# A new prologue, later expert pairs, other places for the routing sums and a split last out-projection in an attention and MoE kernel

## The reference, cut to what matters

```
xn = layernorm(x)
attn: q, k, v = xn @ W + b; softmax(causal(q k^T / sqrt(128))) v @ W_O + b_O
ffn:  r = rmsnorm(xn, ln1_w); q, k = rope(r @ wq), rope(r @ wk); v = r @ wv
      resid2 = xn + attention(q, k, v) @ wo
      xf = rmsnorm(resid2, ln2_w); probs = softmax(xf @ gate_w.T)
      sel = top_k(probs + bias_e, 4); rw = probs[sel] / max(sum(probs[sel]), 1e-12)
      ffn = resid2 + sum_e rw_e * (silu(xf @ weg_e) * (xf @ weu_e)) @ wed_e + shared expert
out = x + attn + ffn
```

## Time and profile before

| what | us |
|---|---|
| three runs | 790.8, 795.21, 793.09 (median 793.09) |
| profiled execution, its own time | 791.5 |
| its span, first to last instruction | 789.7 |
| TensorE busy | 738.3 |
| VectorE, ScalarE, GpSimd busy | 548.8, 490.2, 477.8 |

### The profile page before, as it was taken

The page is one execution under the profiler, slowest core; times in us unless marked ns, Lnnn a source line. Parts: engine busy times, 40 slices in busy tenths (PEclk is TensorE's granted clock), DMA queues, the critical chain, the costliest instruction groups (busy, mean ns, idle before and its releaser), DMA issues.

```text
span 789.7 us, 14401 instructions
## 1 busy us (share of the span) xinstructions
PE 738.3 (93%) x4629; PEld 661.2 (84%) x4629; DVE 548.8 (69%) x1689; ACT 490.2 (62%) x1230; POOL 477.8 (60%) x552
## 2 busy tenths in 40 slices
PE   1899999999999999999988995999999999999995
PEld 1678888888888888989877885999999999999995
DVE  5878888797878887675788763555555655555575
ACT  3777768777777775666434662556655566555652
POOL 3679676776867684327223774566556675665543
PEclk9999999999999999999999997999999999999999
DMA  5000000100010099201000534566797677776351
GB/s 170 27 15 28 14 15 15 34 15 21 24 45 28 14 308 295 73 14 42 14 28 14 184 110 130 128 142 157 165 266 159 162 163 162 176 173 142 68 133 54
DMA packets 103491, 77.51 MB, mean 98 GB/s; under 512 B 6950, under 2 KB 102266, under 8 KB 103418
## 3 DMA queue, kind: packets, MB, share of 16 engines
q1 hardware_dynamic: 92234, 63.19, 28.1%
q0 software_dynamic: 10752, 12.74, 9.7%
q10 hardware_dynamic: 432, 0.67, 0.3%
HBM read 51.75 MB, written 24.82 MB: 97 GB/s over the span
## 4 chain that ended last, share of the span: by engine, by line
PE 64%; DVE 13%; ACT 9%; POOL 7%; issue 4%; DMA 2%; DVEq 0%; SPq 0%; POOLq 0%; ACTq 0%
PE j L820 17%; PE zb L820 8%; PE ob L820 8%; PE s L820 8%; PE t L955 6%; ACT probs L1103 4%; POOL x_slots_dram L686 4%; PE j L909 4%; DVE probsT L1383 3%; PE zb L909 2%; PE ob L909 2%; PE j L917 2%; ACT rope_swapped L1143 2%; ACT rope_swapped L1144 2%; DVE rope_sum L1415 1%
## 5 line engine op out<-in xcount | busy, mean ns | idle before, releaser
L675 POOL TENSOR_SCALAR probs<-probs,inv_sum 128x128 f32<-128x128 f32 x244 | 141.8, 592 | 166.9 <-DVE inv_sum L1374 162.9
L1103 ACT ACTIVATE probs<-probs,neg_max 128x128 f32<-128x128 f32 (+3 forms) x256 | 143.1, 560 | 126.4 <-DVE neg_max L1368 124.9
L820 PE MATMUL s<-k_heads,q_heads 128*128 128x256 f32 (+2 forms) x576 | 138.1, 360 | 3.4 <-DVE neg_max L1368 2.8
L1368 DVE CUSTOM_DVE_ANT_0 probs<-s,mask 128x128 f32<-128x128 f32 (+3 forms) x256 | 119.9, 484 | 11.7 <-PE s L820 6.6
L711 POOL DMA_INDIRECT moe_sum_dram<-late,slot_tokens x64 | 101.4, 1584 | 38.7 <-ACT late L1188 25.7
L1383 DVE TENSOR_TENSOR probsT<-t,probsT 128x384 fp32r<-128x384 f32 (+2 forms) x192 | 101.1, 547 | 12.7 <-ACT probsT L1118 11.9
L1118 ACT ACTIVATE probsT<-t 128x384 fp32r<-128x384 f32 (+2 forms) x192 | 89.8, 486 | 19.4 <-PE t L955 19.3
L955 PE MATMUL t<-ident,probs 128*128 128x128 f32 x640 | 94.3, 274 | 7.8 <-POOL probs L675 6.5
L820 PEld LDWEIGHTS s<-k_heads,q_heads 128*128 128x128 f32 x576 | 90.9, 189 | 10.2 <-DVE neg_max L1368 6.6
L955 PEld LDWEIGHTS t<-ident,probs 128*128 128x128 f32 x640 | 74.9, 140 | 16.6 <-POOL probs L675 8.6
L820 PE MATMUL zb<-probsT,v_heads 128*128 128x512 f32 (+2 forms) x351 | 68.3, 339 | 1.4 <-DVE probsT L1383 0.9
(11 more groups left out here) (251 smaller groups left out, 1576.9 us busy)
## 6 DMA issues: line engine op xcount, KB each, us to landing
x_slots_dram<-mask SPq DMA_DIRECT2D x1, 8480.0 KB, 38.3
late<-x_slots_dram SPq DMA_DIRECT2D x32, 265.0 KB, 4.5
late<-in_L_ffn_weg_dram SPq DMA_DIRECT2D x64, 128.0 KB
late<-in_L_ffn_weu_dram SPq DMA_DIRECT2D x64, 128.0 KB
late<-in_L_ffn_wed_dram SPq DMA_DIRECT2D x64, 128.0 KB
moe_sum_dram<-mask SPq DMA_DIRECT2D x2, 1152.0 KB, 8.8
raw_qk<-in_L_ffn_wq_dram SPq DMA_DIRECT2D x16, 128.0 KB, 2.2
raw_o<-in_L_ffn_wo_dram SPq DMA_DIRECT2D x8, 256.0 KB, 2.6
```

The lines of the kernel that those rows point to most:

```text
L675: pool.tensor_scalar(piece, piece, rinv[:, u % 2, i:i + 1], 1.0, ALU.mult, ALU.mult).then_inc(p_norm, 1)
L820: m = pe.matmul(dst, lhs(a), rhs(b), start=first and i == 0, stop=last_ and i == 2, skip_group_check=skip)
L1103: act.activation(piece, piece, ACT.Exp, bias=nmax[:, u % 2, i:i + 1], scale=-1.0, accum_out=rsum[:, u % 2, i:i + 1]).then_inc(e_done, 1)
L1368: ve.tensor_tensor_reduce(pr[:, u % 2, P_OFF[i]:P_OFF[i] + width], bS[i % 2][:, 0:width], mask_t[:, S - width:S], INV_SCALE, BIG, ALU.add, ...
```

## The change

**Prologue.** SP loads x of batch 0, then the weights of keys and values, then x of batch 1; the small rows are issued by ACT, ahead of the rotary table. The second norm's scale is written in closed form from the first variance, so one power per batch gives the rows; DVE writes those of batch 0, POOL those of batch 1. The squares by ACT are gone there. xn itself is made by POOL in units 0, 1, 4 and 5 (two tiles each) and transposed one unit after (`XN`, four transposes a chunk). The bias is added in units 9 and 17. ACT loads its exponential table early by a one-element activation. In units below 30 DVE takes the values' chunk after the rotary sum and masks the fourth row earlier. PE has nothing to do until the small rows are in; a constant WARM is defined and not used.

**Routing.** DVE no longer makes a table of masked weights. The match of tokens and experts is made at the head of `route_3` in unit 39, POOL multiplies it with the probabilities (`choice`), and DVE sums, normalises and writes the weights in `route_0` of unit 40. POOL makes the constants (`triangle`). `route_1` and `route_2` are called after the chunks of queries and keys and after `z_part`. ACT scales the probabilities in unit 40 too.

**Experts.** DENSE and MOE are one unit later; SENT is as before.

**End.** Out-projection 63 is made in unit 62 and added after the low parts there. The last two are split by head: head 0 before the last attention, head 1 after it. The expert sums of batch 1 are added on PE by products with the identity (plain fp32) into the same banks. The loads of the sums are split by batch, batch 1 first.

```diff
+    XN_UNITS = (0, 1, 4, 5)
...
+            if n in XN_UNITS:
+                found.append(("XN", XN_UNITS.index(n)))
...
-    DENSE, MOE = HALF + 8, HALF + 12
+    DENSE, MOE = HALF + 9, HALF + 13
...
-    ACT_NORMS = (HALF + 9, HALF + 10, HALF + 11)
+    ACT_NORMS = (HALF + 8, HALF + 9, HALF + 10, HALF + 11)
...
-            for b in range(B):
-                sp.dma_start(accB[:, b * TB:(b + 1) * TB, :], xv[:, b * TB:(b + 1) * TB, :]).then_inc(x_in[b], 16)
+            sp.dma_start(accB[:, 0:TB, :], xv[:, 0:TB, :]).then_inc(x_in[0], 16)
...
-            for which in kinds:
+            load("KV", 0, 0)
+            sp.dma_start(accB[:, TB:2 * TB, :], xv[:, TB:2 * TB, :]).then_inc(x_in[1], 16)
+            for which in kinds[1:]:
...
-            for j in range(2):
-                sp.wait_ge(y_out[j], 16 * (PAIRS - SHARED))
-                sp.dma_start(macc[j], moe_sum[j][P:P + B * S, :].rearrange("(t p) d -> p t d", p=P)).then_inc(acc_in, 16)
+            for b in reversed(range(B)):
+                for j in range(2):
+                    sp.wait_ge(y_out[j], 16 * (PAIRS - SHARED))
+                    sp.dma_start(macc[j][:, b * TB:(b + 1) * TB, :],
+                                 moe_sum[j][P + b * S:P + (b + 1) * S, :].rearrange("(t p) d -> p t d", p=P)
+                                 ).then_inc(acc_in[b], 16)
...
+            def first_powers(b):
 
                 ts = slice(b * TB, (b + 1) * TB)
-                pool.wait_ge(ln_step, LN["var", w, b])
-                pool.tensor_tensor(rstd[:, w, ts], var[:, w, ts], mhalf_t[:, ts], ALU.pow).then_inc(ln_pow, 1)
+                pool.wait_ge(ln_step, LN["var", b])
+                pool.tensor_tensor(rstd[:, 1, ts], var[:, 1, ts], mhalf_t[:, ts], ALU.pow).then_inc(ln_pow, 1)
+                pool.wait_ge(ln_pow, b + 1)
+
+            def second_rows(tiles):
+
+                for t in tiles:
+                    pool.tensor_scalar(xr[1][:, t - TB, :], accB[:, t, :], mv[:, t, 0:1], rstd[:, 1, t:t + 1],
+                                       ALU.subtract, ALU.mult).then_inc(rows_of_b1, 1)
+
+            def normal_power():
+
+                pool.wait_ge(ln_step, LN["eps", 1])
+                pool.tensor_tensor(rstd[:, 0, :], var[:, 0, :], mhalf_t[:, :], ALU.pow).then_inc(ln_pow, 1)
+                pool.wait_ge(ln_pow, B + 1)
+
+            def normal_rows(n):
+
+                if n in XN_UNITS:
+                    p = XN_UNITS.index(n)
+                    for t in (2 * p, 2 * p + 1):
+                        pool.tensor_scalar(accA[:, t, :], accB[:, t, :], mv[:, t, 0:1], rstd[:, 0, t:t + 1],
+                                           ALU.subtract, ALU.mult).then_inc(normal, 1)
...
+            def triangle(n):
+
+                if n == LOGITS:
+                    pool.wait_ge(merged, 2)
+                    pool.wait_ge(rows_scaled, NT)
+                    pool.tensor_scalar(before_t, mask_t[:, S - P:S], -1.0, 1.0, ALU.is_lt, ALU.mult).then_inc(ones_done, 1)
+                    pool.memset(ones_t, 1.0).then_inc(ones_done, 1)
+                    for i in range(2):
+                        pool.memset(run[i][:, 0:E], 0.0).then_inc(ones_done, 1)
+
+            def choice(n):
+
+                if n == RANKS + 1:
+                    pool.wait_ge(chosen_done, 1)
+                    pool.tensor_tensor(match, match, route[:, 0, :, 0:E].unsqueeze(2).to_broadcast([P, NT, TOPK, E]),
+                                       ALU.mult).then_inc(weighed, 1)
...
+                triangle(n)
                 send_rows(n)
                 for job in jobs_of(n)[1 if n == -2 else len(first_jobs):]:
-                    if n == -2 and job[0] == "Q2":
+                    if n == -2 and job[0] == "Q3":
+                        first_powers(1)
                         q_sin(n, it)
+                        second_rows(range(TB, TB + 2))
                         q_lo(n, it)
+                        second_rows(range(TB + 2, NT))
                     weights(job, it)
+                choice(n)
                 if n == -1:
                     q_sin(n, it)
                     normalise(n, it)
                     q_lo(n, it)
-                if n in (1, 2):
+                    normal_power()
+                normal_rows(n)
+                if n in (GS + 1, 2 * GS + 1):
                     pool.wait_ge(bc_in, 32)
+                    pool.wait_ge(normal, NT)
                     half = NT // 2
-                    tiles = accB[:, (n - 1) * half:n * half, :]
+                    tiles = accB[:, (n // GS - 1) * half:n // GS * half, :]
                     pool.tensor_tensor(tiles, tiles, bO_t[:, :].unsqueeze(1).to_broadcast([P, half, D]),
                                        ALU.add).then_inc(bias_added, 1)
...
+                elif kind == "XN":
+                    pe.wait_ge(normal, 2 * v + 2)
+                    for k in range(KD):
+                        for j in range(2):
+                            m = pe.transpose(dst[:, (k * 2 + j) * P:(k * 2 + j + 1) * P],
+                                             accA[:, 2 * v + j, k * P:(k + 1) * P], ident[:, :])
...
-                    pe.wait_ge(rt, RT_ONES)
+                    pe.wait_ge(ones_done, 4)
...
+            def add_experts(n):
+
+                o = n - 2
+                half, b = o % 2, o % GS // 4
+                pe.wait_ge(acc_in[b], 32)
+                for t in range(2):
+                    for j in range(2):
+                        pe.matmul(bR[BANK["O", n]][:, t * D:(t + 1) * D], ident[:, :], macc[j][:, b * TB + 2 * half + t, :],
+                                  start=False, stop=False, skip_group_check=True)
...
-                        turn_xr(1)
                         pe.wait_ge(x_lo, KD)
                         for i in range(TB):
                             scores(0, i, it)
                         pe.wait_ge(cx_ev, 1)
-                        turn_xn(0)
+                        turn_xr(1)
                         project(("Qrope", 2), it)
-                        pe.wait_ge(x_lo, 2 * KD)
                         for c in range(2):
                             turn_probs(0, c, it)
-                        turn_xn(1)
                     return
...
+                    if n == UNITS - 1:
+                        last_unit()
+                        return
...
+                    if n == UNITS - 2:
+                        out_project(n + 1, 0, it)
+                        out_project(n + 1, 1, it)
...
+            def last_unit():
+
+                for t in range(2):
+                    out_project(UNITS, t, None, (0,))
+                turn_probs(UNITS - 1, 2, None)
+                for t in range(2):
+                    out_project(UNITS + 1, t, None, (0,))
+                attend(UNITS - 1, None)
+                for n in (UNITS, UNITS + 1):
+                    add_experts(n)
+                for n in (UNITS, UNITS + 1):
+                    for t in range(2):
+                        out_project(n, t, None, (1,))
+
             windows(pe, step)
-            for n in (UNITS, UNITS + 1):
-                out_project(n, 0, None)
-                out_project(n, 1, None)
...
+            act.activation(nmax_t[:, 0:1], mhalf_t[:, 0:1], ACT.Exp).then_inc(table_in, 1)
...
+                did(ve.tensor_scalar(var[:, 1, ts], mv[:, ts, 1], 1.0 + 1e-06, 1e-11, ALU.mult, ALU.add), "var", b)
+                did(ve.tensor_scalar(var[:, 0, ts], mv[:, ts, 1], 1e-05, None, ALU.add), "eps", b)
+
+            variances(0)
+            ve.wait_ge(ln_pow, 1)
+            for t in range(TB):
+                did(ve.tensor_scalar(xr[0][:, t, :], accB[:, t, :], mv[:, t, 0:1], rstd[:, 1, t:t + 1],
+                                     ALU.subtract, ALU.mult), "xr", t)
...
             turned(xrT, 0, 0, bS, L1)
-            first_rms(1)
+            variances(1)
...
                         _, q1, vx = chs
-                        chunk(q1, it)
                         mask_scores(0, 0, it)
                         mask_scores(0, 1, it)
-                        turned(xrT, 1, KD, bT, L1, [0])
+                        chunk(q1, it)
                         mask_scores(0, 2, it)
                         mask_scores(0, 3, it)
-                        for i in range(3):
-                            invert(0, i, it)
-                        turned(xrT, 1, KD, bT, L1, range(1, KD))
+                        invert(0, 0, it)
+                        invert(0, 1, it)
+                        chunk(vx, it)
+                        invert(0, 2, it)
+                        rope_sum(q1, it)
                         invert(0, 3, it)
-                        rope_sum(q1, it)
-                        chunk(vx, it)
-                        turned(xnT, 0, B * KD, (bank["zb"], bank["ob"]), None)
+                        turned(xrT, 1, KD, (bank["ob"], bank["zb"]), L1)
                         probs_lo(0, 0, it)
                         probs_lo(0, 1, it)
```

(46 more changed lines are left out.)

173 lines of the change are left out of this document (74 added, 99 removed).

## The result

The changed kernel takes 795.43 us (median of 20 runs, 794.08 to 797.29) beside 792.55 for the kernel before, run next to it: ratio 1.0041, 95% interval 1.0029 to 1.0052. The forecast was 780, range 774 to 787. The sign was wrong too, though the loss is small. The profiled execution has a span of 795.5 us, beside 789.7 before.

The account below looks back on a forecast made before the run. PE, busy 738.3 of 789.7 us, was taken as the bound, leaving 51 us of idle time to win. Start -5.1, routing and pairs -8.6 and end +0.5 sum to -13.2 off 793.1: 779.9, put at 780, range 774 to 787.

Parts of the forecast that it names:

- Start, forecast -5.1: Prologue and first units: unit 1 starts at 39.9 instead of 47.03 (-7.1), +2.0 given back; bounds -3 and -7.5.
- to POOL, four of some 0.5: Prologue: the second batch's four row tiles move to POOL at some 0.5 us each.
- a wait for POOL's two rows: Unit 1: PE's wait for two rows, counted with four transposes, a copy and a subtraction in +0.9.
- the 43 that was to show the forecast wrong: Test at the start: the forecast is wrong if unit 1 starts after 43 us.
- the 2.0 that the step gave back: Units behind the prologue: transposes in units 1, 2, 5, 6 and moved bias sums cost +2.0 in sum.
- a rival in unit 40 (0.17): Unit 40: waits of 3.0 and 2.9 halve the clock, at most 5.1 us lost, time 784; chance 0.17.
- Routing and pairs, forecast -8.6: Units 36 to 44 and 60: routing work taken off DVE and expert pairs one unit later, together -8.6 us.
- -0.3 to routing: Units 36 to 40: DVE's relief mostly eaten by a new wait in unit 40; -0.3 us, bounds -3 and +2.
- -8.3 to the pairs: Units 44 and 60: the move saves 8.8 of wait and 2.1 at half clock, less 2.6; -8.3 us.
- End, forecast +0.5: Last units: head split and expert sums by identity products on PE end at 790.2 instead of 789.7; bounds -1 and +1.5.
- The slower one: Unit 40: POOL's product with two broadcast operands, at 15.6 us no gain, at 20 ending at 797.5; chance 0.03.
- the 0.93 for faster: Whole kernel: chance 0.93 of a time below 789.1 us; same 0.04, slower 0.03.

Follow-up runs that it names:

- e10b: Changed kernel with the XN transposes a unit later and additions instead of subtractions in POOL's row tiles: 796.73 us beside 807.34 for the kernel before, ratio 0.9877.
- e1_turn_later: Changed kernel with the XN transposes a unit later, POOL's row tiles left in their units: 775.87 us, ratio 0.9803 to the kernel before.
- e6: Changed kernel with the XN transposes a unit later and dense and expert pairs back at units 40 and 44: 777.90 us, ratio 0.9822 to the kernel before.
- e2_pairs_later: Kernel before with only the dense and expert pairs one unit later: 787.63 us beside 792.97, ratio 0.9917.

## Why the prediction was wrong

**Start, forecast -5.1, came out at +16.6.** This is the step that failed, and with it the forecast. Two of its terms were wrong. The second batch went "to POOL, four of some 0.5", and for XN's pairs the step had only "a wait for POOL's two rows" in a term of +0.9. The 0.5 came from no row of a subtraction, and the tiles took 1.21 (pairs) and 1.36 (second rows). Worse, I asked what the tiles cost POOL and not when they were done: they stand last in POOL's unit and their readers first in PE's next. That made four waits, 14.8 us, and the slowed matmuls after them. Unit 1 started at 48.68, past the 43 that was to show the forecast wrong. The way to the first projection was right: x landed at 4.80 (forecast 4.8), the first projection started at 12.85 (12.7), as the changed kernel's timeline has it:

```profile
4.80 1.41 DVE L1397 BATCH_NORM_STATS2 ln_stats<-acc_b 128x6 f32<-128x256 f32 x4 [4.80 <-DMA acc_b<-in_L_attn_x_dram]
...
12.85 2.90 PE L862 MATMUL j<-xrT,w_kv 128*128 128x512 f32 x6 [0.95 <-POOL w_qk L690]
```

And with place and price mended (e10b) unit 1 starts at 39.86, forecast 39.9. With the place alone mended (e1_turn_later), unit 36 starts 5.1 us earlier than before. That this is the forecast's number is luck: unit 1 starts at 42.06, 2.1 late, and the 2.0 that the step gave back in the units behind it did not come (units 1 to 35 took 315.9 us, 316.0 before; 315.0 in e10b).

**Half clock.** I had it as a rival in unit 40 (0.17), from unit 44 of the kernel before. It came there too (clock 0.90 in unit 40, behind the wait of 4.0) but cost most in the first units, where I forecast short waits at most. The window 56.8:63.7 holds PE busy for 3.87 of 6.90 us at a granted clock of 0.65, that is mostly 1.2 GHz. The Trainium skill, TensorE: Matmul & The Clock Gate, section "HAM oscillation — how this bites in real kernels", says that the work behind a long enough TensorE gap runs cold. By that rule, the trace agrees behind these waits, though not behind each: from 80.28 to 93.07 PE stood still for 3.25 us and the clock stayed at 1.00.

**Routing and pairs, forecast -8.6.** In e1_turn_later units 36 to 44 and 60 give -11.1; 3.2 of it is the missing half clock of the kernel before in the stretch with the logits, which comes and goes by itself (below), so -7.9: right in size. The split was wrong. I gave -0.3 to routing and -8.3 to the pairs. Within e6 the routing takes 8.3 off unit 44 and adds 3.0 in units 37 to 40, so -5.3, and the move adds only -2.5 in the trace. I had written that rows are ready 5 us sooner, and did not ask what that does in the old place. The wait in unit 40 came, 4.0 instead of the 3.0 forecast, with POOL's product at 2.34 (forecast 2.40); the second wait forecast there, 2.9 before the transposes, did not come:

```profile
441.02 2.49 PE L862 MATMUL s<-k_heads,q_heads 128*128 128x384 f32 x6 [4.00 <-DVE neg_max L1438]
```

**End, forecast +0.5, came out at -0.2.** The products with the identity took 3.62 us (forecast 3.7). But set against the old end with late pairs, as the one trace of e2_pairs_later has it, the new end is worth 5. The step compared only with the old end as it was with the pairs in their old place.

**The rivals.** The slower one was POOL's product of two broadcast operands. The right engine, the wrong instruction: I looked for danger in an operand form seen nowhere, and took for known a form of TENSOR_SCALAR, with subtraction, that POOL did nowhere in the kernel before either. No rival had the start lose time; the 0.93 for faster rested on that. Two slips in the sums changed nothing: 5.1 over 779.9 is 785, not 784, and the -4.5 at the high end of the range is not what the bounds give (-8.3 + 2 = -6.3).
